# Attention sums sent through DRAM undivided and divided in the experts' front, on one Trainium2 core

## What is computed

```python
attn = softmax(scores)                              # exp(s) / sum of exp(s) over the keys
out = einsum('bhts,bhsd->bhtd', attn, v)            # 8 features for each head
out = out.transpose(0, 2, 1, 3).reshape(b, t, d)    # 16 heads x 8 features = 128
x = layernorm(x + einsum('btd,ed->bte', out, Wout))
```

## Time and profile before

| what | value |
|---|---|
| median of three runs | 1921.84 us (1921.54 to 1922.84) |
| the profiled execution, its own time | 1922.64 us |
| its span, first to last instruction | 1920.8 us |
| PE busy | 1743.9 us, 91% |
| DVE busy | 1389.2 us, 72% |
| ACT busy | 1162.8 us, 61% |
| POOL busy | 97.0 us, 5% |
| mean granted TensorE clock | 0.961 |
| moved by DMA | 68.99 MB, mean 36 GB/s |
| the chain that ended last | PE 70%, DVE 12%, ACT 9% of the span |

### The profile page before, as it was taken

How to read it: one execution, slowest core, us unless ns; L and a number is a source line. 1 busy time by engine, 2 the same in 40 slices (tenths; PEclk the granted TensorE clock), 3 DMA queues, 4 the chain that set the end, 5 groups by cost and what they waited for, 6 DMA issues and landing times.

```text
span 1920.8 us, 31169 instructions
## 1 busy us (share of the span) xinstructions
PE 1743.9 (91%) x9328; PEld 844.8 (44%) x9328; DVE 1389.2 (72%) x2540; ACT 1162.8 (61%) x1801; POOL 97.0 (5%) x123
## 2 busy tenths in 40 slices
PE   6899999699999999579999999999999968988997
PEld 3334343366656656333333333333333325544553
DVE  3788888757777777478889888989898814455544
ACT  3888888544344444107777777777777754444443
POOL 1000000001111011010000000000000000011000
PEclk9899999889999999859999999999999988999999
DMA  7532121101111000210000000000100010000000
GB/s 220 140 92 60 49 62 47 66 1 34 33 33 33 29 10 28 66 41 22 22 23 21 22 21 21 22 22 21 37 26 21 2 44 1 6 6 11 5 5 11
DMA packets 44844, 68.99 MB, mean 36 GB/s; under 512 B 15952, under 2 KB 25056, under 8 KB 44144
## 3 DMA queue, kind: packets, MB, share of 16 engines
q1 hardware_dynamic: 44784, 68.28, 11.9%
HBM read 42.04 MB, written 26.21 MB: 36 GB/s over the span
## 4 chain that ended last, share of the span: by engine, by line
PE 70%; DVE 12%; ACT 9%; issue 5%; SPq 1%; DMA 1%; POOL 1%; DVEq 1%; ACTq 0%; POOLq 0%
PE full_o L689 13%; PE score L676 12%; PE hid_pair L960 11%; PE bank L1060 9%; ACT probs L738 6%; PE causal_o L451 5%; PE triple L435 4%; PE max_pair L652 3%; DVE cprobs L514 2%; PE bank L969 2%; PE bank L990 2%; DVE hid L1317 1%; PE bank L890 1%; PE max_pair L663 1%; DVE negmax L776 1%
## 5 line engine op out<-in xcount | busy, mean ns | idle before, releaser
L776 DVE TENSOR_REDUCE negmax<-max_pair 128x1 f32<-128x1024 f32 x512 | 599.9, 1218 | 69.4 <-PE max_pair L652 62.3
L738 ACT ACTIVATE probs<-score 128x512 f32<-128x512 f32 x1024 | 529.0, 603 | 150.8 <-PE score L676 150.8
L652 PE MATMUL max_pair<-k_st,q_st 64*128 64x512 f32 x1024 | 405.3, 474 | 22.2 <-DMA q_st<-q_scr 18.1
L676 PE MATMUL score<-q_st,k_st 64*128 64x512 f32 x1024 | 382.9, 451 | 34.0 <-ACT probs L738 24.6
L676 PEld LDWEIGHTS score<-q_st,k_st 64*128 64x128 f32 x1024 | 170.6, 185 | 304.7 <-ACT probs L738 284.9
L484 ACT ACTIVATE cprobs<-triple 128x1536 f32<-128x1536 f32 x192 | 268.5, 1456 | 38.5 <-PE triple L435 38.3
L689 PE MATMUL full_o<-probs,v_st 128*32 128x512 f32 x2048 | 272.9, 606 | 0.0
L960 PE MATMUL hid_pair<-x_hi,w_hi 128*128 128x512 f32 x384 | 206.8, 539 | 0.0
L652 PEld LDWEIGHTS max_pair<-k_st,q_st 64*128 64x128 f32 x1024 | 171.7, 191 | 79.5 <-DVE negmax L776 39.5
L1132 ACT ACTIVATE act_s<-hid_pair 128x512 f32<-128x512 f32 x128 | 76.4, 597 | 157.5 <-PE hid_pair L960 157.4
L514 DVE TENSOR_SCALAR cprobs<-cprobs 128x1536 f32<-128x1536 f32 (+6 forms) x272 | 163.0, 624 | 0.4 <-ACT cprobs L484 0.4
(11 more groups left out here) (129 smaller groups left out, 1594.0 us busy)
## 6 DMA issues: line engine op xcount, KB each, us to landing
k_st<-k_scr SPq DMA_DIRECT2D x64, 128.0 KB, 2.8
q_st<-q_scr SPq DMA_DIRECT2D x128, 64.0 KB, 2.3
q_st<-q_scr SPq DMA_DIRECT2D x16, 512.0 KB
k_st<-k_scr SPq DMA_DIRECT2D x64, 104.0 KB
q_scr<-qk_hi SPq DMA_DIRECT2D x24, 256.0 KB, 2.9
k_scr<-qk_hi SPq DMA_DIRECT2D x24, 256.0 KB, 3.1
q_scr<-qk_lo SPq DMA_DIRECT2D x16, 256.0 KB, 2.9
k_scr<-qk_lo SPq DMA_DIRECT2D x16, 256.0 KB, 3.2
```

Of the source, the lines that this page charges most:

```text
L652: ins = nc.tensor.matmul(ring[slot][:, half, :], q_st[p][rows, qt * P:(qt + 1) * P], k_st[p][rows, j, half * CH:(half + 1) * CH], start=Tr ...
L676: nc.tensor.matmul(sbank[L.score_bank(e)][:, :], k_st[p][rows, j, kt * P:(kt + 1) * P], q_st[p][rows, q0:q0 + w], start=True, stop=True, t ...
L738: nc.scalar.activation(probs[s % NP][:, j, :], sbank[L.score_bank(e)][:, :], ACT.Exp, scale=SCALE).then_inc(L.exp_done, 1)
L776: nc.vector.tensor_reduce(negmax[:, qt // TPC, j, qt % TPC:qt % TPC + 1], ring[slot][:, :, :].rearrange("p a n -> p (a n)"), AXX, ALU.max, ...
```

## The change

The turning and the division leave both attentions. A finished bank is still copied to SBUF, but to one of two buffers `o_sb[0]` and `o_sb[1]`, one per chunk, and SP stores it to DRAM (`o_scr`) as it is, features on partitions, sums among them. The causal attention gets a second accumulator bank, where `spare` was, so each chunk has its own. In the experts' front SP loads eight feature rows of each head into `o_raw` and the sum row of each head, repeated eight times, into `o_sum`; DVE takes the reciprocal of all 128 x 512 of them and multiplies into `ot`. The copy L1270, the turns L890 of `os_` and ACT's copy L1098 go. `o_tm`, `os_` and `o_rcp` are gone; `w_raw` has a place of its own, so its loads stand earlier in SP's order: `w1`, `w2` and the rotation tables in the causal attention, `we1` and `we2` just ahead of the full attention's first stacks. Each copy out of the bank now waits for the store of the round before from the same buffer (`o_kept`).

```diff
         def dve_save_o(dve, L, i, qc, blocks):
             dve.wait_ge(L.pv_done, blocks)
-            if not isinstance(chunk, int) or chunk > 0:
-                dve.wait_ge(L.spare_ready, chunk)
-            nc.vector.tensor_copy(o_sb[:, :], causal_o[:, :]).then_inc(L.o_saved, 1)
+            if not isinstance(i, int) or i > 0:
+                dve.wait_ge(L.o_kept[qc], 16 * i)
+            nc.vector.tensor_copy(o_sb[qc][:, :], causal_o[qc][:, :]).then_inc(L.o_saved, 1)
...
         def pe_slot_values(pe, L, i, p, n):
-                    if qc > 0 or not isinstance(i, int) or i > 0:
-                        pe.wait_ge(L.o_saved, CPB * i + qc)
+                    if not isinstance(i, int) or i > 0:
+                        pe.wait_ge(L.o_saved, CPB * (i - 1) + qc + 1)
...
         def pe_round(pe, L, i, p, nxt):
-                if prev and n == L.NORM_PREV:
-                    pe_norm(pe, L, CPB * i - 1, 2 * i - 1)
-                if n == L.NORM_0:
-                    pe_norm(pe, L, CPB * i, 2 * i)
...
+        def sp_keep_o(sp, L, i, qc):
+            b, g = bg(i)
+            sp.wait_ge(L.o_saved, CPB * i + qc + 1)
+            sp.dma_start(o_scr[L.n][bass.ds(b, 1), bass.ds(g, 1), :, qc * CH:(qc + 1) * CH].rearrange(
+                "b g c n -> (b g c) n"), o_sb[qc][:, :]).then_inc(L.o_kept[qc], 16)
+
+        def sp_load_o(sp, st, L, b, hh):
+            sp.wait_ge(L.o_kept[hh], 16 * G * (b + 1))
+            heads = o_scr[L.n][bass.ds(b, 1), :, :, hh * CH:(hh + 1) * CH].rearrange(
+                "b g (j r) n -> (b g j) r n", j=HG)
+            sp.dma_start(o_raw[:, :], heads[:, 0:DK, :]).then_inc(st.o_loaded, 16)
+            sp.dma_start(o_sum[:, :], heads[:, DK:DK + 1, :].broadcast_to([H, DK, CH])).then_inc(st.o_loaded, 16)
...
         def sp_causal(sp, L):
+            sp_keep_o(sp, L, 0, 0)
             sp.wait_ge(L.scores_ready, L.N)
             sp_load_causal(sp, L, 2, 0)
             sp_store_pads(sp)
+            sp_keep_o(sp, L, 0, 1)
+            sp_keep_o(sp, L, 1, 0)
...
+            sp_keep_o(sp, L, 1, 1)
+            for k, name in enumerate(("w1", "w2")):
+                sp.dma_start(w_raw[k][:, :], d[name]).then_inc(raw_loaded[k], 16)
+            sp.dma_start(rope_a[:, :], d["rope_a"]).then_inc(rope_loaded, 16)
+            sp.dma_start(rope_b[:, :], d["rope_b"]).then_inc(rope_loaded, 16)
+            sp_keep_o(sp, L, 2, 0)
             with sp.Fori(1, NG // 2 - 1) as u:
                 for k in range(2):
                     i = 2 * u + 2 + k
                     sp.wait_ge(L.scores_ready, L.N * (i - 1))
                     sp_load_causal(sp, L, i, k)
+                    sp_keep_o(sp, L, i - 2, 1)
+                    sp_keep_o(sp, L, i - 1, 0)
...
         def act_save_o(act, L, i, qc, s):
             act.wait_ge(L.pv_done, NP + i * L.S + s + 1)
-            if qc == 1 or prev:
-                act.wait_ge(L.ring_ready, norm_turned(L, i, qc, prev, nxt))
-            nc.scalar.activation(o_sb[:, :], full_o[:, :], ACT.Copy).then_inc(L.o_saved, 1)
+            if not isinstance(i, int) or i > 0:
+                act.wait_ge(L.o_kept[qc], 16 * i)
+            nc.scalar.activation(o_sb[qc][:, :], full_o[:, :], ACT.Copy).then_inc(L.o_saved, 1)
...
         def dve_beside(dve, st, n, back, front, par, layer):
                 if n == pl.o_turn - 1:
-                    nc.vector.tensor_copy(os_[:, :, :], o_tm[:, bass.ds(front * TPC, TPC), :]).then_inc(st.o_in, 1)
+                    dve.wait_ge(st.o_loaded, 2 * 16 * (front + 1))
+                    nc.vector.reciprocal(o_sum[:, :], o_sum[:, :]).then_inc(st.o_rcp, 1)
+                    dve.wait_ge(st.o_rcp, front + 1)
+                    nc.vector.tensor_tensor(ot[:, :], o_raw[:, :], o_sum[:, :], ALU.mult).then_inc(st.ot_ready, 1)
...
         def pe_beside(pe, st, n, back, front, par, layer):
-                if n == pl.o_turn:
-                    pe.wait_ge(st.o_in, front + 1)
-                    pe_turn_tiles(bank[3], os_).then_inc(st.o_turned, 1)
...
+            sp.dma_start(w_raw[0][:, :], d["we1"]).then_inc(raw_loaded[0], 16)
+            sp.dma_start(we2[:, :, :], d["we2"]).then_inc(we2_loaded, 16)
             sp_full(sp, layers[1])
-            sp.wait_ge(layers[1].normed, CPB * NG)
-            sp.dma_start(w_raw[0][:, :], d["we1"]).then_inc(raw_loaded[0], 16)
-            sp.dma_start(we2[:, :, :], d["we2"]).then_inc(we2_loaded, 16)
```

More of the change, by code:

```diff
@@ L99, in __init__ @@
         self.o_saved = sem("l0_o_saved")
-        self.spare_ready = sem("l0_spare_ready")
-        self.spare_free = sem("l0_spare_free")
-        self.chain = sem("l0_chain")
-        self.normed = sem("l0_normed")
+        self.o_kept = [sem(f"l0_o_kept{h}") for h in range(CPB)]
     def order_of(self, n):
@@ L152, in __init__ @@
         self.chain = sem("l1_chain")
-        self.normed = sem("l1_normed")
+        self.o_kept = [sem(f"l1_o_kept{h}") for h in range(CPB)]
     def values_before(self, i):
@@ L158, in ring_base, with ring_slot @@
     def ring_base(self, i):
-        if isinstance(i, int) and i == 0:
-            return self.FIRST
-        return (PAIRS + 2) * i + self.FIRST - 1
-    def ring_slot(self, i, k):
-        return (self.FIRST + k) % 2 if isinstance(i, int) and i == 0 else (self.FIRST - 1 + k) % 2
+        return PAIRS * i + self.FIRST
+    def ring_slot(self, k):
+        return (self.FIRST + k) % 2
     def score_bank(self, e):
@@ L216, in build_program @@
         with ExitStack() as overlay:
-            causal_o = overlay.enter_context(nc.psum_tensor("causal_o", [P, CH], F32))
-            spare = overlay.enter_context(nc.psum_tensor("spare", [P, CH], F32))
+            causal_o = [overlay.enter_context(nc.psum_tensor(f"causal_o{h}", [P, CH], F32)) for h in range(CPB)]
             triple = [overlay.enter_context(nc.psum_tensor(f"triple{i}", [P, 3, CH], F32)) for i in range(2)]
@@ L245, in build_program @@
         v_all = sb("v_all", [P, NT, D])
-        o_tm = sb("o_tm", [P, NT, D])
+        o_sb = [sb(f"o_sb{h}", [P, CH]) for h in range(CPB)]
+        o_raw = sb("o_raw", [P, CH])
+        o_sum = sb("o_sum", [P, CH])
+        w_raw = [sb(f"w_raw{k}", [P, NH * P]) for k in range(2)]
+        xt = [sb(f"xt{i}", [P, CH]) for i in range(2)]
+        xt2 = xt[1]
+        qk_hi = [sb(f"qk_hi{i}", [P, CH]) for i in range(4)]
+        qk_lo = [sb(f"qk_lo{i}", [P, CH]) for i in range(4)]
+        with ExitStack() as overlay:
+            rh = overlay.enter_context(nc.sbuf_tensor("rh", [P, 2, CH], F32))
+            we2 = overlay.enter_context(nc.sbuf_tensor("we2", [P, NH, P], F32))
+        rope_a = sb("rope_a", [P, T])
+        rope_b = sb("rope_b", [P, T])
+        rot = [sb(f"rot{i}", [P, CH]) for i in range(4)]
         st6 = sb("st6", [P, 2, TPC, 6])
@@ L280, in build_program @@
         with ExitStack() as overlay:
-            w_raw = [osb(f"w_raw{k}", [P, NH * P]) for k in range(2)]
             w_hi = [osb(f"w_hi{k}", [P, NH * P], F32R) for k in range(2)]
@@ L317, in build_program @@
         k_scr1 = nc.dram_tensor("k_scr1", [B, H, 3 * DK + 2, T], F32, kind="Internal").ap()
+        o_scr = [nc.dram_tensor(f"o_scr{n}", [B, G, P, T], F32, kind="Internal").ap() for n in range(2)]
         aug_scr = nc.dram_tensor("aug_scr", [2, CPB, P, SLOT], F32, kind="Internal").ap()
@@ L416, in rows_of @@
             return r, slice(r, r + ROWS)
-        def pe_norm(pe, L, chunk, job):
-            pe.wait_ge(L.o_saved, chunk + 1)
-            if not isinstance(job, int) or job > 0:
-                pe.wait_ge(L.spare_free, job)
-            for t in range(TPC):
-                last = nc.tensor.transpose(spare[:, t * P:(t + 1) * P], o_sb[:, t * P:(t + 1) * P], ident[:, :])
-            last.then_inc(L.spare_ready, 1)
         def pe_slot_scores(pe, L, i, p, n):
@@ L656, in pe_half_pair @@
                 ins.then_inc(L.ring_ready, 1)
-        def pe_full_norm(pe, L, chunk, pos, slot):
-            pe.wait_ge(L.o_saved, chunk + 1)
-            pe.wait_ge(L.ring_free, pos - 1)
-            for t in range(TPC):
-                last = nc.tensor.transpose(ring[slot][:, 0, t * P:(t + 1) * P], o_sb[:, t * P:(t + 1) * P],
-                                           ident[:, :])
-            last.then_inc(L.ring_ready, 1)
         def pe_score(pe, L, i, p, e):
@@ L1095, in act_beside @@
             if front is not None:
-                if n == pl.o_turn:
-                    act.wait_ge(st.o_turned, front + 1)
-                    nc.scalar.activation(ot[:, :], bank[3][:, :], ACT.Copy).then_inc(st.ot_ready, 1)
                 if n == pl.x_turn:
@@ L1426, in _ @@
                 sp.sem_inc(st.done, 1)
+            with sp.Fori(0, B // 2) as b:
+                for hh in range(2):
+                    c = 2 * b + hh
+                    store_out(c)
+                    sp.wait_ge(st.ot_ready, c + 3)
+                    sp_load_o(sp, st, layers[1], b + 1 + hh, 1 - hh)
+            for c in range(B, 2 * B):
+                store_out(c)
```

(3 more changed lines are left out.)

189 lines of the change are left out of this document (70 added, 119 removed).

## The result

The changed kernel takes **1929.3 us** (median of six runs, 1928.1 to 1934.1) against 1922.6 us of the kernel before on the same chip: ratio 1.0044, 95% interval 1.0031 to 1.0057. It is slower by 0.4%, where the forecast was 0.2% faster (1919). The time lies inside the range, 1902 to 1938, on the side that was given 0.34.

A forecast was written before the change was run, and what follows sets the result against it. PE was taken to set the pace of both attentions. Terms -25.1 - 26.5 + 14.7 + 12.9 + 16.7 + 2.4 + 1.5 gave -3.4 us against 1922.64; with the median 0.8 lower, 1919 us, 8-in-10 range 1902 to 1938.

The forecast's parts named there:

- The queue in the causal attention: Causal attention, round 2: 3 MB of loads ahead of a store and round 4's stacks cost +1.5 us, between 0 and +4.
- The prelude of the full attention: Before the full attention: we1 and we2, 2 MB ahead of the first stacks, delay them by 2.4 us, between 0 and +5.
- The clock: Both experts' stages: longer PE waits drop the granted clock to 0.50 nearly every time, +16.7 us, between 0 and +25.
- The stages' hold: Experts' fronts: reciprocal and multiply hold DVE 3.5 us longer, PE waits for hid; +14.7 us first stage, +12.9 second.
- Causal: Causal attention: turns and the wait for the bank's copy leave PE, 1.62 us a round over 15.5 rounds, -25.1 us.
- the second bank: Causal attention: with two accumulator banks PE no longer waits for the copy, 0.44 us a round.
- the turns and divisions: Causal attention: two groups of four turns leave PE, 0.59 us each on the chain, 1.18 us a round; DVE loses two divisions.
- Full: Full attention: removing the turns and their ring slot saves 1.66 us a round over 16 rounds, -26.5 us.
- The reciprocal: Experts' fronts: DVE's 128x512 reciprocal takes 3.18 us, from two smaller forms; bounds 0.69 and 4.4 us.
- Rival 3: Experts' fronts: the reciprocal takes 4.4 us, 1.24 more each, +18.6 us, total 1937 us; chance 0.10.
- Rival 1: Experts' stages: long waits leave the clock alone and DVE's detour is partly hidden, total 1902 us; chance 0.22.
- Rival 2: Experts' stages: slower, the clock stays low after each fall, two low stretches a chunk, about +17, 1936 us; chance 0.15.

The follow-up runs named there:

- experiment 2: Changed kernel with w1, w2, the rotation tables, we1 and we2 issued near the attentions' ends instead of ahead of their rounds: 1919.3 us, ratio 0.9989 to the kernel before.
- experiment 1: Changed kernel with the reciprocal of o_sum replaced by a plain copy of o_sum onto itself: 1868.6 us, ratio 0.9726 to the kernel before.
- half_width: Changed kernel with the reciprocal over only the first 256 of 512 columns: 1888.4 us (two runs), ratio 0.982 to the kernel before.
- reciprocal_in_before: Kernel before with one added DVE reciprocal of 128x512 unused values behind the copy to os_ in the front: 1966.5 us, ratio 1.0227 to the kernel before.

## Why the prediction was wrong

Its mechanisms all happened. About 57 us leave the attentions and about 62 come back in the experts' stages and on the queue, where some 52 and 48 were forecast. The step that failed is the size of what comes back: the terms of the queue, of the clock and of the hold in the experts' stages were all too small.

**The queue in the causal attention failed: "+1.5 us, between 0 and +4", because the loads come "a full round ahead of need".** It is 6.5 us (experiment 2). The text counted 3 MB and one landing of 9.2 us. It did not count that `w3` (1 MB, issued at 107.92) and the small weights go out a few us ahead of them, nor that the clock falls behind the wait; how the 6.5 us divide between these was not tried. A time from issue to landing that was read from a quiet stretch is no bound for a crowded one: the same `rope_b` lands 11.5 us after its issue now (DMA issues of 60 to 175 us: KB each, us to landing):

```profile
rope_b<-in_rope_b SPq DMA_DIRECT2D x1, 512.0 KB, 11.5
```

The prelude of the full attention, +2.4, is 3.8; with the loads behind instead of ahead it is 1.3 in one profile (53.2 less 51.9).

**The clock, +16.7, was too small: 19.8.** Its part of the first stage, 7.8, is 10.1 in PE's busy time (experiment 1); its part of the second, 8.9, is 9.7. That PE would idle 3.3 us at step 8 and the clock fall nearly each time is as forecast (3.23 us; one fall in each of the six chunks, from 452.7 to 729.1 us).

**The stages' hold, 14.7 and 12.9, was too small by less.** The two stages grew by 27.4 and 24.6 us where 22.5 and 21.8 were forecast with the clock. Without the clock's 10.1 and 9.7 that leaves 17.3 and 14.9 for the hold. The rule behind the two terms was nearly right. In the first stage the product of step 8 starts 3.80 us after that of step 7 before the change (460.74 to 464.54) and 6.26 us after it now (445.36 to 451.62): 2.46 us more, forecast 2.3, and the reciprocal's own 0.16 us is the difference. To subtract the 1.24 us of slack of the kernel before was therefore right, since the forecast compared the start of the product before and after. PE's wait of 3.23 us is longer than what the chunk pays, because PE comes there earlier, without the turns and their wait. In the second stage the same distance goes from 3.81 (1682.32 to 1686.13) to 6.25 us (1672.22 to 1678.47): 2.44 more, forecast 2.1. There the reason given was wrong and the number nearly right by luck: the `hid` in question comes ahead of POOL's wait in DVE's order, and what covers a part of the hold is 1.26 us of PE's slack, about as much as the 1.4 us that were subtracted. Six chunks of these differences make 1.0 of the 2.6 us by which the first stage's hold was missed, and all of the second's 2.0. The other 1.6 us were not taken apart.

**The attentions gave more, which hid part of the miss.** Causal: -27.4 without the queue's term, forecast -25.1. A round gives 1.79 us, of which 0.33 is the second bank (forecast 0.44) and 1.46 the turns and divisions (forecast 1.18 for two groups on the chain). Full: -29.7, forecast -26.5; 2.01 us a round, forecast 1.66. The full price of a group of turns is more than its 0.59 us and its slot in the ring; what more was not tried.

**The reciprocal, 3.18 us, is 3.34.** The line through two small forms was 5% low. Rival 3, 4.4 us by a repeat count of 8, falls. Rival 1 falls too, since the clock did drop. Rival 2's sign came true, and a part of its way: in the second stage the granted clock is at 0.50 for 37.5 us in eight stretches, two of them in each of two chunks, where the kernel before has 10.2 us in three. But what they cost is in the 9.7 us above, far from the +17 of the rival, and in the first stage there is one stretch a chunk.

Against the forecast of -3.4, the mean column has +5.2. The queue's two terms make +6.4 of the 8.6 between, the experts' stages +7.7, and the attentions give 5.5 back.

## What to carry to other kernels

When work is moved onto an engine that another one waits for, compare when the waiting instruction starts before and after, and subtract the slack of the kernel before once. The wait that the new profile shows can be longer than what is paid, when the change also removes work ahead of it. Ask of such work first whether it can be cut into pieces no longer than the room in a step, or done before its values are spread (64 columns for 512): here the pieces, in one of two stages, turned a change which loses 0.4% into one that gains 1.2%, and the small reciprocal together with the late loads gained 3.5%. Loads that nobody needs for long belong behind the ones that somebody does, and their price is in the bytes in front of the next needed transfer.

## What the runs showed of the hardware

The reciprocal on VectorE takes 249 ns for 16 columns, 546 for 64, 1189 for 168, 1737 for 256 and 3336 for 512: about 0.15 us and 6.2 ns a column, six times the 1.04 ns of a two-input operation. The Trainium skill, page "VectorE: DVE Perf Modes", section "Walkthrough: the 8-slice pipeline in each mode", gives the reciprocal a repeat count of 8. An estimate from that figure, 8 times 1.04 ns, would be 8.3 ns a column; no form here shows that.

In the first experts' stage PE's granted clock stays at 1.00 in all six chunks when PE's wait for `hid` is 1.63 us (`half_width`). It falls to 0.50, the 1.2 GHz level, in five of six with waits of 1.85 to 1.88 us (`reciprocal_in_before`), and in all six with waits of 3.23 us in the changed kernel. Behind the wait in the long causal round it is at 0.50 for 6.8 us.

Eleven profiles with the same code up to the attention began `causal_o` between 59.0 and 64.7 us. So 5 us in one profiled execution need have no cause in the code; a second profile tells.
